# Sliding-window attention and trigonometric FFN on 8 cores: both scores groups and AV of a head pair adjacent, transposes of P on one PSUM bank

## The reference, cut to what matters

```python
NUM_HEADS, WINDOW = 16, 256          # D = 1024, Dh = 64, nb = 2048 / 256 = 8 blocks
q, k, v = proj(wq), proj(wk), proj(wv)                  # (x @ w.T), by block and head
k2 = concat([k of the previous block, k of this one]);  v2 = the same of v
scores = einsum('bhjqd,bhjkd->bhjqk', q, k2) / sqrt(Dh)
scores = where(band & kpos_ok, scores, neg)             # 256 keys seen by each query
out = einsum('bhjqk,bhjkd->bhjqd', softmax(scores), v2) @ wo.T
# layer
x = x + layernorm(attn(layernorm(x)))
h = layernorm(x)
real, imag = h @ cos(theta + theta_noise), h @ sin(phi + phi_noise)
x = x + layernorm(sqrt(real * real + imag * imag))
```

## Time and profile before

| | |
|---|---|
| time, median of 3 runs | 2736.85 us (2734.85 to 3174.53) |
| the profiled execution's own time | 2736.3 us |
| its span on the slowest core (core 0) | 2734.7 us; the eight cores 2724.3 to 2734.7 |
| PE busy | 2610.6 us, 95% |
| DVE, ACT, POOL busy | 46%, 32%, 19% |
| PE's share of the chain that ended last | 86% |
| mean granted TensorE clock, core 0 | 0.984 |

### The profile page before, as it was taken

How to read it: one execution, slowest core, us unless ns; L and a number is a source line. 1 busy time by engine, 2 the same in 40 slices (tenths; PEclk the granted TensorE clock), 3 DMA queues, 4 the chain that set the end, 5 groups by cost and what they waited for, 6 DMA issues and landing times.

```text
span 2734.7 us, 46503 instructions; the slowest of 8 cores (2724.3 to 2734.7 us)
## 1 busy us (share of the span) xinstructions
PE 2610.6 (95%) x16923; PEld 1576.1 (58%) x17088; DVE 1253.0 (46%) x2564; ACT 885.6 (32%) x2061; POOL 515.8 (19%) x676
## 2 busy tenths in 40 slices
PE   7899999999999998989999999999999999999998
PEld 6556575757465656656575757566644444444443
DVE  5445444445454444344444444444454443443442
ACT  4324342424242424233232323232333222221221
POOL 0112131222122122212121212212122110111111
PEclk9999999999999999999999999999999999999999
DMA  7111212212121221212101010202322433423332
GB/s 249 63 29 57 55 55 57 62 53 70 39 70 40 70 59 51 63 48 61 32 32 32 32 39 25 63 1 63 124 62 93 116 85 108 116 80 113 107 83 58
DMA packets 173777, 185.68 MB, mean 68 GB/s; under 512 B 131824, under 2 KB 132080, under 8 KB 173040
## 3 DMA queue, kind: packets, MB, share of 16 engines
q1 hardware_dynamic: 173552, 182.69, 22.9%
HBM read 109.25 MB, written 41.94 MB: 55 GB/s over the span
## 4 chain that ended last, share of the span: by engine, by line
PE 86%; DVE 5%; issue 4%; ACT 3%; DMA 2%; SPq 0%; DVEq 0%; ACTq 0%; POOL 0%; POOLq 0%
PE pb L653 24%; PE pb L287 18%; PE pb L328 13%; PE pb L362 12%; PE pb L427 7%; PE pb L504 5%; PE pb L468 5%; PE pb L562 2%; DVE stats L444 1%; DVE pb L442 1%; DMA r_sb<-thb 1%; DVE x_sb L190 1%; ACT p_sb L447 1%; DMA r_sb<-phb 1%; SPq L59 0%
## 5 line engine op out<-in xcount | busy, mean ns | idle before, releaser
L287 PE MATMUL pb<-xth,wreg 128*128 128x256 bf16 x3840 | 704.4, 276 | 27.5 <-ACT k_sb L306 27.5
L456 POOL TENSOR_SCALAR p_sb<-p_sb,stats 128x384 f32<-128x384 f32 (+2 forms) x512 | 339.1, 674 | 1382.9 <-DVE stats L452 776.5
L447 ACT ACTIVATE p_sb<-pb,stats 128x384 f32<-128x384 f32 (+2 forms) x512 | 286.2, 560 | 785.5 <-DVE stats L444 743.3
L287 PE MATMUL pb<-xtl,wreg 128*128 128x256 bf16 x1920 | 527.8, 275 | 0.0
L287 PEld LDWEIGHTS pb<-xth,wreg 128*128 128x128 bf16 x3840 | 378.2, 98 | 141.2 <-issue 94.3
L442 DVE TENSOR_TENSOR pb<-pb,mask_s 128x256 f32<-128x256 f32 (+1 forms) x512 | 209.9, 410 | 365.7 <-PE pb L427 365.5
L328 PE MATMUL pb<-wreg,xth 128*128 128x512 bf16 x979 | 309.5, 395 | 47.5 <-ACT q_sb L306 23.4
L653 PE MATMUL pb<-wreg,q_sb 128*128 128x512 bf16 x1505 | 331.2, 379 | 1.6
L362 PE MATMUL pb<-wreg,aoh 128*128 128x512 bf16 x995 | 302.1, 379 | 3.6 <-issue 2.4
L653 PE MATMUL pb<-wreg,xth 128*128 128x512 bf16 x1002 | 300.8, 379 | 1.5 <-issue 0.6
L444 DVE TENSOR_REDUCE stats<-pb 128x1 f32<-128x384 f32 (+2 forms) x512 | 272.8, 533 | 53.4 <-DVE pb L442 0.9
(11 more groups left out here) (63 smaller groups left out, 2505.4 us busy)
## 6 DMA issues: line engine op xcount, KB each, us to landing
x_sb<-x SPq DMA_DIRECT2D x64, 512.0 KB, 5.5
r_sb<-x SPq DMA_DIRECT2D x32, 512.0 KB, 5.2
x<-r_sb SPq DMA_DIRECT2D x32, 512.0 KB, 2.7
wreg<-x SPq DMA_DIRECT2D x32, 512.0 KB, 8.5
y<-wreg SPq DMA_DIRECT2D x64, 256.0 KB, 2.3
trig<-o_sb SPq DMA_DIRECT2D x32, 256.0 KB, 3.0
wreg<-trig SPq DMA_DIRECT2D x4, 2048.0 KB, 19.4
wreg<-wkT SPq DMA_DIRECT2D x4, 1024.0 KB, 14.1
```

What stands on the lines that cost most here:

```text
L287: e.matmul(bank[b][:, 0:256], a, r, start=s, stop=z)
L447: texp = ac.inc(lambda e, e2=e2, pu=pu, sc=sc: e.activation(pu, sc, AF.Exp, bias=stats[:, col + e2:col + e2 + 1], scale=1.0, accum_out=sta ...
L456: tok["p", e2, qs] = po.inc(lambda e, e2=e2, pu=pu: e.tensor_scalar(pu, pu, stats[:, col + 4 + e2:col + 5 + e2], 1.0, op0=ALU.mult, op1=AL ...
```

## The change

Scores get four banks (2 to 5) instead of three, and the transposes one (6) instead of two. `scores` now issues the matmuls of both halves at once (`score_mm`), then mask, maximum and exponential of three heads, the scaling of half 0, the fourth head and the scaling of half 1. `transposes` treats one head of one half, so that a head pair has four groups of three transposes, all through bank 6, with a dense step behind each. Then come scores of the next head pair, AV, and the remaining steps. V's steps are half as long and twice as many. Chains in `later` are cut differently: `ln_x` takes the ACT half of a layer-norm application out of the item that applies it (still seven items), and a `trig_chunk` has seven items instead of four, queued once at the end of `s` = 2.

```diff
-        DB, SB, TB, AB = (0, 1), (2, 3, 4), (5, 6), 7
+        DB, SB, TB, AB = (0, 1), (2, 3, 4, 5), 6, 7
...
             parts = [lambda: stat(0), lambda: stat(1), rstd, lambda: app(0), lambda: app(1)]
-            return parts + [lambda: low(0), lambda: low(1)] if split else parts
+            if not split:
+                return parts
+            return parts[:4] + [lambda: (app(1), high(0)), lambda: (high(1), low(0)), lambda: low(1)]
...
-            return [lambda k2=k2: step(k2) for k2 in range(4)]
+            return [lambda kc=kc: step(kc) for kc in range(8)]
...
+        def scores(g, hp):
+            for qs in range(2):
+                score_mm(g, hp, qs)
+            softmax_head(g, hp, 0, 0)
+            softmax_head(g, hp, 0, 1)
+            softmax_head(g, hp, 1, 0)
+            softmax_scale(g, hp, 0)
+            softmax_head(g, hp, 1, 1)
+            softmax_scale(g, hp, 1)
...
+        def transposes(g, hp, qs, e2):
             ps = tiles(g, qs)
             c0 = ps[0] * 128
-            for e2 in range(2):
...
+            u = unit(e2, qs)
+            pe.wait(tok["p", e2, qs], *bfree[TB])
...
-            return [lambda: trig_load(which, kc, a, b), lambda: None,
-                    lambda: trig_sum(which, a, b), lambda: trig_pair(which, kc, b)]
+            return [lambda: trig_load(which, kc, a, b), lambda: None, lambda: None,
+                    lambda: trig_sum(which, a, b), lambda: trig_sin(which, a, b),
+                    lambda: trig_high(b), lambda: trig_low(which, kc, b)]
...
         for f in range(4):
-            xt_fill(f, ())
+            xt_fill(f, SB[f], ())
...
-                per = {4: [1, 1, 1, 1, 0], 5: [1, 1, 1, 1, 1], 6: [1, 1, 1, 1, 2],
-                       7: [1, 2, 1, 1, 2]}.get(len(dense), [2, 2, 2, 2, 2])
-                if len(dense) == 4 and s in (2, 3, 4, 5, 6):
-                    per = [1, 1, 1, 0, 1]
-                transposes(g, s, 0)
-                go(per[0])
-                fill(0)
-                nxt(0)
-                go(per[1])
-                transposes(g, s, 1)
-                go(per[2])
-                fill(1)
-                nxt(1)
-                go(per[3])
+                per = {14: [2, 2, 2, 2], 8: [1, 1, 1, 1], 7: [1, 1, 1, 1], 6: [1, 1, 1, 1],
+                       5: [1, 1, 1, 1], 4: [1, 1, 0, 1]}.get(len(dense), [1, 1, 1, 1])
+                for n, (qs, e2) in enumerate(((0, 0), (0, 1), (1, 0), (1, 1))):
+                    transposes(g, s, qs, e2)
+                    go(per[n])
+                    if n == 1:
+                        fill(0)
+                    elif n == 3:
+                        fill(1)
+                if s < 7:
+                    scores(g, s + 1)
+                elif not last:
+                    scores(g + 1, 0)
+                evict = attend(g, s)
+                if s > 1:
+                    evict()
+                run(dense, len(dense) - 3)
+                if later:
+                    later.pop(0)()
+                run(dense, 1)
                 fill(2)
+                run(dense, 2)
                 fill(3)
...
-                evict = attend(g, s)
-                if s > 1:
-                    evict()
-                go(per[4])
...
-                if s in (3, 4) and g > 0:
-                    t0 = (g - 1) * tpp + (s - 3) * (tpp // 2)
-                    for i in range(t0, t0 + tpp // 2):
-                        if i < 2 * KC:
-                            later += trig_chunk(i)
+                if s == 2 and g > 0:
+                    for i in range((g - 1) * tpp, min(g * tpp, 2 * KC)):
+                        later += trig_chunk(i)
```

More of the change, by code:

```diff
@@ L312, in v_steps, with step @@
             st = {}
-            def step(k2):
-                if k2 == 0:
+            def step(kc):
+                if kc == 0:
                     st["b"] = (dense_bank(), dense_bank())
                     pe.wait(*tok["w", 2], *bfree[st["b"][0]], *bfree[st["b"][1]])
-                pe.wait(*tok["xt", 0, k2])
+                pe.wait(*tok["xt", 0, kc // 2])
                 last = [None, None]
[L320 to L334, removed]
+                for tt in range(2):
+                    b = st["b"][tt]
+                    xh = xth[:, kc * 256 + tt * 128:kc * 256 + (tt + 1) * 128]
+                    xl = xtl[:, kc * 256 + tt * 128:kc * 256 + (tt + 1) * 128]
+                    for i, (a, r) in enumerate(three(xh, xl, wh(2, kc, nh * 512, 512),
+                                                     wl(2, kc, nh * 512, 512))):
+                        f = lambda e, a=a, r=r, b=b, s=(kc == 0 and i == 0), \
+                            z=(kc == 7 and i == 2): e.matmul(bank[b][:], a, r, start=s, stop=z)
+                        if i == 2:
+                            last[tt] = pe.inc(f)
+                        else:
+                            pe.do(f)
+                tok["v_pe", kc // 2] = last[1]
+                if kc == 7:
                     for tt in range(2):
@@ L402, in unit, with score_mm @@
             return (2 * e + qs) * 384
-        def scores(g, hp, qs):
+        def score_mm(g, hp, qs):
             j0 = g % nblk == 0
[L407 to L410, removed]
+            c0 = tiles(g, qs)[0] * 128
+            sbk = SB[2 * qs:2 * qs + 2]
             pe.wait(tok["kq", 0, g, hp], tok["kq", 1, g, hp], *bfree[sbk[0]], *bfree[sbk[1]])
@@ L429, in scores, with softmax_head @@
             tok["s", g, hp] = t
+            tok["s", qs] = t
+        def softmax_head(g, hp, qs, e2):
+            c0 = tiles(g, qs)[0] * 128
             col = (hp % 2) * 12 + qs * 6
-            two = c0 == 0
-            texp = None
-            dv.wait(t, t_const)
-            for e2 in range(2):
[L435 to L450, removed]
@@ L456, in scores @@
                 tok["p", e2, qs] = po.inc(lambda e, e2=e2, pu=pu: e.tensor_scalar(
                     pu, pu, stats[:, col + 4 + e2:col + 5 + e2], 1.0, op0=ALU.mult, op1=ALU.mult))
-        def transposes(g, hp, qs):
+        def scores(g, hp):
[7 more added lines that the diff above has]
+            softmax_scale(g, hp, 1)
@@ L763, in build_nc @@
         steps = v_steps(0, 0)
-        run(steps, 2)
-        scores(0, 0, 0)
-        scores(0, 0, 1)
-        run(steps, 2)
+        run(steps, 4)
+        scores(0, 0)
+        run(steps, 4)
         later = []
@@ L804, in fill @@
                     if s == 0 and g == 0 and NB > 1:
-                        xt_fill(f, [tok.get(("v_pe", f))])
-                def nxt(qs):
-                    if s < 7:
-                        scores(g, s + 1, qs)
-                    elif not last:
-                        scores(g + 1, 0, qs)
+                        xt_fill(f, TB, [tok.get(("v_pe", f))])
                 def go(n):
```

95 lines of the change are left out of this document (57 added, 38 removed).

## The result

The changed kernel takes **2671.23 us** (median of four executions, 2670.65 to 2844.28); the kernel before, measured beside it, had a median of 2764.39 us. Compared execution by execution the ratio is **0.9763, 95% interval 0.9735 to 0.9791**: 2.4% faster. To an outcome faster by over 2%, as it came, the forecast gave only 0.30.

A forecast was written before the change was run, and what follows sets the result against it. PE, busy for 95% of the span, was taken to bound the kernel. From 2736.3 us, -48 - 29 - 16 + 12 + 19 + 4 + 12 + 4.5 + 0.7 = -41 gave 2695 us, range 2655 to 2728.

The forecast's parts named there:

- Form changes, -48: PE's scores and AV: adjacent halves save 0.29 us in 128 pairs (37 us), AV's entry 0.09 us 127 times (11.5 us).
- The start of `s` = 7: V's wait behind the Q eviction on ACT falls from 3.05 to 1.1 us, 15 times: -29 us.
- PE sees it 0.35 later: Delay assumed from the end of an ACT eviction or copy until PE goes on: 0.35 us.
- Half clock: 1.2 GHz stretches behind 23 long waits cost 1.25 us each; 13 at s = 7 go: -16 us, trig's stay.
- V behind V, +12: V's next group at s = 7 waits 0.78 us for both banks, 15 times: +12 us, bounds 0 to 1.11 each.
- From `s` = 1 into 2: Transposes wait for the single bank's ACT copy (+0.45 us) and DVE copy (+0.9 us), 14 times: +19 us.
- Trig: Blocks 1 to 8: sines and table loads ahead of copies cost 5.1 us a block, 41 us against 29 before: +12 us.
- Block 15: PE reaches the transposes before P, 0.6 us five times, and copies stand behind the square-root table: +4.5 us.
- rival 1: The single transposes bank is hardly waited for, half of 52 us added waits go: 2664 us; chance 0.25.
- Rival 2: The drain stays between the two halves' scores, 0.20 us in 128 pairs: +26 us, 2721 us; chance 0.08.
- Rival 3: The clock falls behind shorter waits too, some 20 of 1.1 to 1.4 us: 2736 us; chance 0.08.
- Rival 4: The single bank (bank 6) gates every transposes group: +150 us, 2845 us; chance 0.05.

The follow-up runs named there:

- experiment 1: Changed kernel with one dense step moved between the two halves' scores, except in head pair s = 6; 2708.24 us, ratio 0.9869.
- experiment 2: Changed kernel with one dense step moved between scores and AV; 2684.9, 2685.1 and 2685.9 us, ratio 0.9784.
- experiment 3: Kernel before with only the new `ln_x` cut (ACT halves one item later); 2673.8, 2678.5 and 2692.7 us, ratio 0.9772.
- experiment 6: Changed kernel with V waiting for its second bank only when the first matmul into it comes; 2661.69 us, ratio 0.9701.
- experiment 8: Changed kernel with an empty item ahead of the second tile's `ln_o`, so its statistics come after the s = 2 copy; 2659.2 to 2661.4 us, ratio 0.9666.
- experiment 4: Changed kernel with each sine or cosine of the FFN weights computed twice in place; 2696.7 to 2699.2 us, ratio 0.9831.
- experiment 7: Changed kernel with the sum and sine of each block's first trig chunk one item earlier; 2647.2 and 2649.5 us.
- experiment 9: Changed kernel with V's bank-by-bank wait, the earlier sine and the later `ln_o` statistics all together; 2617.7 and 2618.75 us, ratio 0.9542.
- experiment 5: Kernel before, its order and banks kept, with the new `ln_x` and `trig_chunk` cuts; 2646.03 us in the profiled execution, ratio 0.9697.
- experiment 10: Kernel before with both chain cuts, AV moved directly behind the second half's scores, and V waiting bank by bank; 2666.9 us, profiled 2689.0 us.

## Why the forecast was 24 us too high

**Form changes, -48.** The mechanism and the size held. 1.49 us for both halves and 1.45 for AV are the sizes forecast, and experiments 1 and 2 gave 28 to 37 and 14 us for the terms of 37 and 11.5. On the Trainium skill's rule (TensorE: Matmul & The Clock Gate, Part 3) the drain of the second half would have stayed, and the scores would have taken about 1.7 us; the trace and experiment 1 decide against it here.

**The start of `s` = 7.** The mechanism held (the second L213 now stands behind the Q eviction), and the wait was 0.69 us from start to start, not 1.1: -6 us. Half of that is the wake-up of the next paragraph. ACT's evictions of 128x256 are spaced 0.26 us (1760.96 to 1761.22), where 0.3 was estimated; what the rest is stays open. Experiment 3 shows the whole term: this cut alone gave some 60 us where the forecast had 29 + 16 = 45.

**The wake-up of PE: read from a row with a matmul missing.** "PE sees it 0.35 later" stands in four of the waits worked out. No row is named for it; it seems to be read from V's row, which starts 0.37 us behind the end of ACT's eviction (1576.45 + 0.36). But ahead of that row stand two weight loads, and the matmul of the first is missing from core 0's record. Core 1 has the same place whole:

```profile
1576.45 0.36 ACT L306 ACTIVATE q_sb<-pb 128x256 f32<-128x256 f32 x1
1576.93 0.13 PEld L328 LDWEIGHTS pb<-wreg,xth 128*128 128x128 bf16 x2 [2.55 <-issue]
1577.18 0.38 PE L328 MATMUL pb<-wreg,xth 128*128 128x512 bf16 x1 [2.56 <-ACT q_sb L306]
```

```profile
1573.61 0.37 ACT L306 ACTIVATE q_sb<-pb 128x256 f32<-128x256 f32 x1
1574.12 0.59 PE L328 MATMUL pb<-wreg,xth 128*128 128x512 bf16 x2 [2.34 <-ACT q_sb L306]
```

From ACT's end (1573.98) to PE's start are 0.14 us, and so they are at nearly every wait for ACT in both traces (625.92 + 0.48 to 626.54 above). The 0.2 us too many stand in each wait for ACT: at `s` = 7 (15 x 0.2 = 3 us), at `s` = 3, 4, 5, where the whole 0.23 us were this error (4 us), and with trig (some 2 us).

**Half clock: the step that failed most.** I gave 15 of the 44 us that the mean clock of 0.984 was short to the start, and so priced a stretch at 1.25 us. The granted clock over the whole span of core 0 of the kernel before shows 22 stretches of 3.42 us at 0.50, 22 x 1.71 = 38 us: 21 behind waits before V and K/Q, one in block 0. The start took 3.5 us, at a third value of 0.81 in 18.7 us, and the end 3, where PE had nothing to run:

```profile
28.52:39.30 10.78, 10.78 (x85) 0.81 0.99 327
...
2728.89:2734.60 5.71, 0.00 (x0) 0.50 0.25 93
```

In the changed kernel a clock of 0.995 is short by 13 us: three stretches behind trig waits, three in block 0 (two of them in one piece, below), together 10 us, and again 3 at the end.

```profile
80.37:87.20 6.83, 5.16 (x15) 0.50 0.95 295
```

So of the stretches that the forecast priced 18 went at 1.71: -31 us instead of -16. The two more in block 0 cost about what the start no longer lost. Two errors add up: the price (1.71 instead of 1.25), and that I let all eight trig waits keep theirs, "since a 2.6 us wait is near the 2.56 us that brought it on". The waits came out at 2.0 to 2.1 us of idle time (1.5 in block 8), and three of eight kept it.

**V behind V, +12.** Held to the digit: 0.78 us, in nearly all of 15 blocks; experiment 6 took it away.

**The single bank.** From `s` = 1 into 2, 0.24 for ACT's copy and 1.09 for DVE's are 1.33 us where 1.35 to 1.4 was forecast. The two parts were forecast at 0.45 and 0.9: the 0.2 us of the wake-up was too much in the first and, since DVE's copy ends when it ends, too little in the second, so that it cancels by luck. Experiment 8 gave 11 us back of DVE's part, 14 x 0.92 = 13 by the idle times. The wait of 0.23 at `s` = 3, 4, 5 without trig does not show: -4. Trig: 4.2 us a block (2.2 + 0.76 + two of 0.35 + two of 0.27), not 5.1: -7. The first wait has the 0.2 us of the wake-up too many; what made the later ones shorter no run isolates. Experiments 4 and 7 show that the first wait is the sine ahead of the copy: a longer sine adds its length, and a sine out of the way takes 16.8 of the 26.4 us. Block 15: waits of some 13 us where about 8 was forecast: +5.

**The sum anew:** -48 - 31, and waits +11 (-35 at `s` = 7, +12, +19, +5 of trig, +10 in block 15) make -68, against a measured -65. Against the forecast: clock -15, waits -12, -27, measured -24. The account closes to 3 us; what those are stays open. That it closes is partly the sum's doing: the waits of block 15 were priced too low and most others too high, and the terms of block 0 and of the start were not measured apart.

**Rivals.** The time lies between the forecast and rival 1 (2664, "hardly waited for"), nearer to its number, but not for its reason: the waits came one by one where they were worked out, mostly smaller, and no run shows one swallowed by another (in experiment 9 the gains of three even add up to more than their sum). Rival 2 is refuted by experiment 1. Rival 3: waits of 1.1 us and less brought no half clock anywhere in the changed kernel. Rival 4: no wait in clean slots; the slack held, which with a wake-up of 0.14 us is 0.4 and not 0.2 us.

**What made the kernel faster** is therefore not the new grouping of PE's work. The cuts of the chains alone gave about 90 us (experiment 5). The grouping saved 48 and, against experiment 5, brought some 72, added up from the changed kernel's waits and not measured one by one: V behind V 12, the statistics ahead of the copy 19, the trig waits 26 (34 us, of which experiment 5 keeps some 8), block 15 10, and three half-clock stretches 5. I had both in one sum, and did not see that they stood against each other.

**Open:** why the same wait of 2.1 us is followed by half clock in three blocks of the changed kernel and in seven of experiments 6 and 8. That is on the slowest cores; the eight cores of one execution run the same program and have it behind two to three of these waits in the changed kernel, three to seven in experiment 6, one to seven in experiment 8. So a difference of some 7 us between two of these kernels can be this alone, and no run here varied it by itself.

## What to carry to other kernels

Before regrouping the busiest engine, look for an eviction that stands in another engine's queue behind an instruction that waits: moving that one instruction (five lines) gave 60 us here, as much as the whole rearrangement, since it took away the wait and the half clock behind it. When a resource is cut from two to one to save form changes (0.25 to 0.33 us a pair), walk the queue of every engine that frees it and move what stands ahead of the copy; done at three places, this turned a net loss of 25 us into a gain of 28. A saved form change must not bring a consumer closer to the copies that it reads: experiment 10 lost more than it saved in that way. And a delay that stands in many terms should be read at several waits and on a core whose matmul count is whole: here one row with a missing record put 0.2 us into each of them.

## What the runs showed of the hardware

- Half clock came behind idle times of 2.13 us, and not always: of four equal waits in the windows above, two. Length alone does not decide. Behind 3.4 us in experiment 4 it came every time (four waits on each of eight cores), but core 3 in experiment 3 was idle for 2.6 to 3.3 us seven times and never had it, while core 0 had it behind all eight of its waits of 2.3 to 4.4 us. The shortest that had it behind them were 1.8 us (experiment 10) and, in block 15 of experiments 3, 5 and 10, 0.6 or 0.8 us with 1.6 us close behind; behind 1.1 us or less alone it never came. A stretch lasted 3.42 us or twice that, and one of 3.42 us cost up to 1.71.
- From the end of ACT's or DVE's instruction to the start of the matmul that waits for it, the traces have 0.14 to 0.15 us (1573.98 to 1574.12; 1699.90 to 1700.05).
- In the same form, scores' second half needs no drain: the eight matmuls of both halves take 1.49 us against 2 x 0.86 apart, and from scores to AV it takes no longer than from scores to dense.
